# Delta rule in a twelve-stage decoder: block products of two units in one step, outputs copied out of PSUM at once, roots for two units together, decays by a scan

## The reference, cut to what matters

```python
q = silu(dwconv_causal(x @ Wq)); k = silu(dwconv_causal(x @ Wk)) * DK**-0.5; v = silu(dwconv_causal(x @ Wv))
alpha = sigmoid(x @ Wa + ba); beta = sigmoid(x @ Wb + bb)
def step(S, inp):                      # one token
    Sk = einsum('bhvk,bhk->bhv', S, kt)
    S = at * S - bt * (Sk - vt)[..., :, None] * kt[..., None, :]
    return S, einsum('bhvk,bhk->bhv', S, qt)
o = layernorm(outs) * sigmoid(x @ Wg)
return o @ Wo
```

## Time and profile before

| | before |
|---|---|
| median of 3 runs (lowest to highest) | 3912.71 us (3912.12 to 3914.6) |
| the profiled execution | 3915.85 us |
| its span | 3913.9 us |
| mean granted TensorE clock | 0.931 of full speed |
| PE busy | 3368.3 us, 86% |
| PEld busy | 2147.7 us, 55% |
| DVE busy | 2962.4 us, 76% |
| ACT busy | 1945.8 us, 50% |
| POOL busy | 1136.4 us, 29% |

### The profile page before, as it was taken

One profiled execution on the slowest core, in us unless ns is written; L12 is line 12 of the kernel. 1 busy time (PEld: TensorE's weight loads), 2 busy tenths in 40 slices (PEclk: granted clock), 3 DMA queues, 4 the chain that ended last, 5 costly groups with the idle time before them and its releaser, 6 DMA issues.

```text
span 3913.9 us, 63880 instructions
## 1 busy us (share of the span) xinstructions
PE 3368.3 (86%) x22787; PEld 2147.7 (55%) x22802; DVE 2962.4 (76%) x6366; ACT 1945.8 (50%) x4750; POOL 1136.4 (29%) x1183
## 2 busy tenths in 40 slices
PE   7799999999886296877989978788999999997765
PEld 3366666666554143664556655465666566664444
DVE  6798999989756867454367766768988888886668
ACT  4466666666552142431144434535666566663455
POOL 1633033215410200000011121113656565664110
PEclk9899999999997598988989998899999999998887
DMA  2222222222211010001000000112222222122000
GB/s 71 58 74 58 69 63 68 57 63 64 48 38 47 0 36 24 2 2 64 1 22 1 1 33 2 60 65 83 77 73 76 75 76 81 66 81 77 1 1 22
DMA packets 240232, 183.97 MB, mean 47 GB/s; under 512 B 117744, under 2 KB 216432, under 8 KB 239024
## 3 DMA queue, kind: packets, MB, share of 16 engines
q1 hardware_dynamic: 239920, 179.90, 15.2%
HBM read 164.61 MB, written 15.20 MB: 46 GB/s over the span
## 4 chain that ended last, share of the span: by engine, by line
PE 63%; DVE 26%; ACT 5%; issue 5%; SPq 0%; DMA 0%; POOL 0%; DVEq 0%; ACTq 0%; POOLq 0%
PE ps L310 22%; PE ps L3286 5%; PE ps L2912 3%; PE ps L3274 3%; PE ps L502 2%; PE ps L2958 2%; PE ps L580 1%; PE ps L2695 1%; DVE hMX L3031 1%; PE ps L3265 1%; PE ps L1972 1%; PE ps L2918 1%; PE ps L2171 1%; DVE daq L732 1%; PE ps L316 1%
## 5 line engine op out<-in xcount | busy, mean ns | idle before, releaser
L310 PE MATMUL ps<-xT,min 128*128 128x512 f32 (+1 forms) x1072 | 496.1, 608 | 11.8 <-DVE macc L3426 11.4
L3426 DVE SCALAR_TENSOR_TENSOR macc<-ps,mcw,macc 128x508 f32<-128x508 f32 (+2 forms) x408 | 302.6, 742 | 80.5 <-ACT macc L3353 70.8
L3527 POOL TENSOR_TENSOR mSQ<-mSQ,mtn 128x512 f32<-128x512 f32 x128 | 234.6, 1833 | 331.2 <-ACT mtn L3378 331.1
L310 PEld LDWEIGHTS ps<-xT,min 128*128 128x128 f32 (+1 forms) x1072 | 191.0, 189 | 228.2 <-issue 205.7
L3520 POOL TENSOR_TENSOR mE<-mE,mCB 128x1024 f32<-128x1024 f32 x128 | 302.2, 2361 | 44.4 <-DVE mE L3436 26.4
L3436 DVE TENSOR_TENSOR_SCAN mE<-mE,mid 128x1024 f32<-128x1024 f32 x128 | 300.1, 2344 | 0.0
L3031 DVE TENSOR_REDUCE hMX<-ps 128x2 f32<-128x512 f32 x256 | 165.4, 686 | 110.3 <-PE ps L2918 109.6
L3286 PE MATMUL ps<-mwo,macc 128*128 128x256 f32 x1024 | 243.0, 380 | 5.4 <-DVE macc L3443 5.3
L3374 ACT ACTIVATE mtn<-ps,mcol 128x64 f32<-128x64 f32 x1024 | 222.9, 334 | 2.8 <-PE ps L3265 2.8
L826 POOL TENSOR_TENSOR dTB<-did,dNB 128x1024 f32<-128x1024 f32 (+1 forms) x10 | 29.1, 2912 | 664.7 <-DMA dNB<-d_N 600.4
L2998 ACT ACTIVATE hE<-ps 128x512 f32<-128x512 f32 x256 | 139.0, 595 | 156.2 <-PE ps L2912 156.2
(11 more groups left out here) (597 smaller groups left out, 8261.2 us busy)
## 6 DMA issues: line engine op xcount, KB each, us to landing
mE<-m_decay SPq DMA_DIRECT2D x128, 512.0 KB, 3.5
dwk<-in_L_attn_Wk SPq DMA_DIRECT2D x64, 128.0 KB, 2.3
dwq<-in_L_attn_Wq SPq DMA_DIRECT2D x64, 128.0 KB, 2.3
dwv<-in_L_attn_Wv SPq DMA_DIRECT2D x64, 128.0 KB, 2.3
dwg<-in_L_attn_Wg SPq DMA_DIRECT2D x64, 128.0 KB, 2.4
dwo<-in_L_attn_Wo SPq DMA_DIRECT2D x64, 128.0 KB, 2.6
min<-in_m_in SPq DMA_DIRECT2D x2, 4096.0 KB, 18.2
d_N<-dNT SPq DMA_DIRECT2D x256, 16.0 KB, 1.5
```

Source lines behind the costliest of these rows:

```text
L310: t = pe.matmul(out, w[:, j, :], self.c.xT[:, j, blk(g, 512)], start=j == 0, stop=j == 1)
L3426: x = dve.scalar_tensor_tensor(out=acc[:, :, 3 - j:T], in0=p[:, :, 0:T - 3 + j], scalar=self.cw[:, i, j:j + 1], in1=acc[:, :, 3 - j:T], op ...
L3527: pool.tensor_tensor(self.SQ[g % 2][:, :], self.SQ[g % 2][:, :], self.tn[s][:, :], ALU.add).then_inc(*self.sqa.up)
```

## The change

- **Decays.** Alpha itself (an exponential) goes to DRAM once; each unit reads its row of 4 x 132 values into all partitions (`decay_in`), ACT scales an identity by beta's part of each column (`seed`), and DVE runs one scan over 528 elements, E(t) = alpha(t) E(t-1) + seed(t). The matmuls L509 and L510, the exponential L643 and the bf16 parts of the sums go.
- **Silu.** ACT takes Silu straight into KQ or av; the DVE step L739 goes. The gate stays a tanh.
- **Block products.** `p32` holds x32 of unit u and y32 of unit u-1, `p64` likewise x64 and y64, their matmuls interleaved. One group of y32 goes to bank 6.
- **Outputs.** `oc` copies bank 4 to SBUF right after `o`; the statistics read SBUF, and `on` works in place there, in a ring of three.
- **Roots.** `st` takes the statistics of each unit; `c1` and `c2` make the roots of two units (eight columns) in one chain, split over two iterations.
- **NB in two buffers.** The load of a batch waits for the batch before the last.
- **The rest.** LAG 13, a ring of 15, 85 iterations in place of 81, V and W in one buffer, the weights of v, gate and Wo in rings of four with a semaphore each, the write-out and read-back of the blocks moved ahead of the late weights in SP's list, the order of steps rewritten.

```diff
-        for t in range(self.U + self.LAG + 5):
-            a, b, v, w, x = t, t - 1, t - self.LAG, t - self.LAG - 1, t - self.LAG - 2
-            every = (("k", a), ("x32", v), ("vt", w), ("on", x), ("q", a), ("k2", a), ("y32", v), ("s0", b), ("w", w), ("s1", b), ("q2", a),
-                     ("v", v), ("x64", v), ("ot", x), ("gate", w), ("v2", v), ("y64", v), ("o", w), ("e", a), ("acc", x), ("close", x),
-                     ("stats", x - 1), ("scale", x - 2), ("turn", x - 3))
+        for t in range(self.U + self.LAG + 8):
+            a, b, v, w, x = t, t - 1, t - self.LAG, t - self.LAG - 2, t - self.LAG - 5
+            every = (("oc", w - 1), ("k", a), ("st", w - 1), ("c1", w - 1), ("c2", w - 2), ("p32", v), ("k1", a), ("on", x), ("q", a), ("vt", w),
+                     ("cols", a), ("s0", b), ("s1", b), ("k2", a), ("p64", v - 1), ("q1", a), ("seed", a), ("v", w + 1), ("ot", x), ("v0", w + 1),
+                     ("go", x), ("w", w), ("q2", a), ("gate", x + 1), ("v1", w + 1), ("e", a), ("acc", x), ("v2", w + 1), ("o", w),
+                     ("close", x), ("stats", x - 1), ("scale", x - 2), ("turn", x - 3))
...
# SP: one iteration of load()
+            if 0 <= b < self.U:
+                for m, u0 in enumerate(self.first):
+                    if b == u0:
+                        self.blocks_out(sp, m)
+                self.blocks_in(sp, b)
...
-                    if m:
-                        sp.wait_ge(*self.sub.at(m))
+            if m >= 2:
+                sp.wait_ge(*self.sub.at(m - 1))
...
+        if n + 4 < self.U:
+            self.decay_in(sp, n + 4)
...
+    def decay_in(self, sp, u):
+        row = self.decd[u // 16, u % 16, :].unsqueeze(0).broadcast_to([128, 528])
+        sp.dma_start(self.E[u % 4][:, :, :].rearrange("p j t -> p (j t)"), row).then_inc(self.e_sem[u % 4], 16)
...
# PE
-            elif step == "e":
...
-                pe.matmul(bank(6), self.sel[:, h:h + 1].broadcast_to([96, 128]), self.S3[:, blk(g, 512)], start=True, stop=False)
-                pe.matmul(g4(bank(6)), c.identb[:, :], bc(c.neg[:, :], 4), start=False, stop=True).then_inc(*self.eb.up)
...
+            elif step == "p64":
+                X, Y = u < self.U, u > 0
+                lo, hi = blk(0, 64), blk(1, 64)
+                if X:
+                    pe.wait_ge(*self.yc32.at(u + 1))
+                if Y:
+                    pe.wait_ge(*self.xc64.at(u))
+                    TT = g4(self.TT[(u - 1) % 4][:, :])
                 for b in range(4):
+                    to = slice(256 + 64 * b, 320 + 64 * b)
+                    if X:
+                        x = pe.matmul(bank(7)[hi, to], self.NT[r][lo, 128 * b + 64:128 * b + 128], self.T[u % 4][lo, b, :], start=True, stop=True)
+                    if Y:
+                        y = pe.matmul(bank(7)[lo, to], self.X2[1 - s][hi, b, :], TT[hi, b, hi], start=True, stop=True)
...
-                room[4] = self.on.at(u + 1)
+                room[4] = self.oc.at(u + 1)
...
# ACT
-                act.activation(self.tk[:, :], self.ak[:, :], ACT.Tanh, scale=0.5).then_inc(*self.hk.up)
+                act.activation(self.KQ[s][:, :, 0, :], g4(self.ak[:, :]), ACT.Silu).then_inc(*self.sk.up)
...
+            elif step == "seed":
                 for j in range(4):
-                    e = act.activation(self.E[s][:, j, 1:129], bank(6)[:, blk(j)], ACT.Exp, bias=self.col[:, 4 * g + j, h:h + 1])
+                    e = act.activation(self.seed[s][:, j, 1:129], c.ident[:, :], ACT.Copy, scale=self.col[:, 4 * g + j, h:h + 1])
...
+            elif step == "oc":
+                act.wait_ge(*self.o.at(u + 1))
+                if u >= 3:
+                    act.wait_ge(*self.ot.at(u - 2))
+                act.copy(self.O[u % 3][:, :], bank(4)).then_inc(*self.oc.up)
...
# DVE
+            elif step == "e":
...
+                dve.wait_ge(self.e_sem[u % 4], 16 * (u // 4 + 1))
+                dve.wait_ge(*self.sd.at(u + 1))
+                dve.tensor_tensor_scan(E, E, seed, 0.0, ALU.mult, ALU.add).then_inc(*self.de.up)
...
+            elif step == "c2":
+                st, (y, v, a) = self.s8[u // 2 % 2], [self.sw[u // 2 % 2][:, blk(i, 8)] for i in range(3)]
+                for _ in range(2):
+                    dve.wait_ge(own.sem, root)
+                    root = self.newton(dve, own, y, v, a)
...
+    def newton(self, dve, own, y, v, a):
+
+        dve.wait_ge(own.sem, own(dve.scalar_tensor_tensor(out=a, in0=y, scalar=-0.5, in1=y, op0=ALU.mult, op1=ALU.mult)))
+        dve.wait_ge(own.sem, own(dve.tensor_tensor(a, a, v, ALU.mult)))
+        return own(dve.scalar_tensor_tensor(out=y, in0=a, scalar=1.5, in1=y, op0=ALU.add, op1=ALU.mult))
...
# POOL
-            then(pool.tensor_tensor(TB, self.id32[0:P], NB.rearrange("p s t -> p t s"), ALU.subtract))
+            then(pool.tensor_scalar(TB, NB.rearrange("p s t -> p t s"), -1.0, 1.0, ALU.mult, ALU.mult))
+            then(pool.memset(TB.rearrange("p t c -> p (t c)")[:, 0:1024:33], 1.0))
```

More of the change, by code:

```diff
@@ new lines, in scores_out @@
+    def scores_out(self, sp, n):
+        m = self.batch[n]
+        sp.wait_ge(*self.nr.at(2 * n + 2))
+        if m >= 2 and n == self.first[m]:
+            sp.wait_ge(self.nb_sem[m % 2], 16 * (m // 2))
+        for k in range(4):
+            to = self.Nd[m % 2, n - self.first[m], :, k, :, :].rearrange("b s t -> s b t")
+            sp.dma_start(to, g4(self.NT[n % self.RING][blk(k, 32), :])[:, :, blk(k, 32)]).then_inc(self.n_sem[m % 2], 16)
+        if n == self.first[m] + self.BATCHES[m] - 1:
+            so_far = sum(self.BATCHES[i] for i in range(m % 2, m + 1, 2))
+            sp.wait_ge(self.n_sem[m % 2], 64 * so_far)
+            if m >= 2:
+                sp.wait_ge(*self.sub.at(m - 1))
+            P = 16 * self.BATCHES[m]
+            of = self.Nd[m % 2].rearrange("u b k s t -> (u b k) s t")[0:P]
+            sp.dma_start(self.NB[m % 2][0:P, :, :], of).then_inc(self.nb_sem[m % 2], 16)
+        if n + 4 < self.U:
+            self.decay_in(sp, n + 4)
@@ L495, in tensor @@
                 self.columns(pe, bank(b), w, g).then_inc(*done.up)
+            elif step == "cols":
+                pe.wait_ge(*room[4])
+                pe.wait_ge(*self.logs.at(1))
+                for j in range(4):
+                    t = pe.transpose(bank(4)[:, blk(j)], self.Bt[:, blk(j)], c.ident[:, :])
+                t.then_inc(*self.ab_tr.up)
+                room[4] = self.cols.at(1)
             elif step in ("s0", "s1"):
@@ new lines, in scalar @@
+                    e = act.activation(self.seed[s][:, j, 1:129], c.ident[:, :], ACT.Copy, scale=self.col[:, 4 * g + j, h:h + 1])
+                e.then_inc(*self.sd.up)
+            elif step == "p32":
+                p = bank(7).rearrange("p (i b n) -> p i b n", i=4, b=4)
+                if u:
+                    act.wait_ge(*self.y32.at(u))
+                if u < self.U:
+                    act.wait_ge(*self.x32.at(u + 1))
+                    act.copy(self.X[s][:, :, :], p[:, 0, :, :]).then_inc(*self.xc32.up)
+                if u:
+                    TT = g4(self.TT[(u - 1) % 4][:, :])
+                    for k in range(2):
+                        lo, hi = blk(2 * k, 32), blk(2 * k + 1, 32)
+                        act.activation(TT[lo, :, hi], p[lo, 0, :, :], ACT.Copy, scale=-1.0)
+                    act.activation(self.T[(u - 1) % 4][32:64, :, 0:32], bank(6)[32:64, 0:128].rearrange("p (b n) -> p b n", b=4), ACT.Copy, scale=-1.0).then_inc(*self.yc32.up)
+            elif step == "p64":
+                p = bank(7)[:, 256:512].rearrange("p (b n) -> p b n", b=4)
+                if u < self.U:
+                    act.wait_ge(*self.x64.at(u + 1))
+                    act.copy(self.X2[s][64:128, :, :], p[64:128]).then_inc(*self.xc64.up)
+                if u:
+                    act.wait_ge(*self.y64.at(u))
+                    act.activation(g4(self.TT[(u - 1) % 4][:, :])[0:64, :, 64:128], p[0:64], ACT.Copy, scale=-1.0).then_inc(*self.yc64.up)
@@ L708, in vector @@
+        then(dve.tensor_scalar(beta, bank(1), self.bia[:, 1:2], 0.0, ALU.add, ALU.min))
         dve.wait_ge(*self.soft.at(2))
-        dve.tensor_tensor(beta, beta, self.Bt[:, :], ALU.subtract)
-        then(dve.tensor_tensor(self.B1[:, :], self.B1[:, :], self.A[:, :], ALU.subtract))
-        for j in range(4):
-            x = dve.tensor_tensor_scan(self.cum[:, blk(j)], self.one[:, :], self.B1[:, blk(j)], 0.0, ALU.mult, ALU.add)
-        then(x)
-        dve.tensor_tensor(self.Bt[:, :], beta, self.cum[:, :], ALU.subtract).then_inc(*self.cummed.up)
```

364 lines of the change are left out of this document (164 added, 200 removed).

## The result

3799.6 us median (3798.3 to 3801.5, 4 runs) against 3912.4 in the same comparison: ratio 0.9711, 95% interval [0.9695, 0.9728]. Forecast 3804. The profiled execution took 3798.25 us, its span 3796.5. Behind the stage, where both kernels are the same, the two profiled executions differ by some 4.5 us (2735.5 from 1178.4 on, 2730.9 from 1065.6 on), so a few us of a single execution are not the change's.

What follows compares the result with a forecast made beforehand. PE bounds with POOL idle, DVE with POOL busy. The stage was to end at 134 + 52 + 6 + 708 + 166 = 1066 us against 1178; with a table load -111, forecast 3804 us, 8 in 10 range 3775 to 3868.

Steps and rivals of the forecast that it cites:

- from there to the first full iteration: After the first block product: five filling iterations, 52 us, plus 6 us of stall because batch 1 comes late from POOL.
- 46 full iterations: Iterations with all steps running: 46 at a mean of 15.4 us against 16.6 before, 708 us.
- tail: Late steps only: 15 iterations of PE's 9.6 plus 0.6 us, 153, then 13 for the last unit; 166 us.
- PE bounds the full iteration: Full iteration: PE's work falls from 16.16 to 15.0 us (14.56 to 15.72), 15.2 with handoffs and POOL idle.
- p64's overlap: Block products on PE: x64 and y64 run side by side, 0.61 us instead of 1.22 per iteration.
- Rival 1: Block products in p64 do not overlap: PE 15.7 us, 16.0 with handoffs, +37 us, 3841; chance 0.16.
- DVE: DVE's load per full iteration: 11.9 us with POOL idle, 13.5 with it busy, so it no longer bounds.
- My walk through the queues: Full iteration with POOL busy: q's copy and waiting for bank 3 make gate 0.9 us late; iteration 15.9 us.
- Front: Opening iterations where DVE sets the pace: still 7.2 us each, iteration 1 some 4 to 7 us earlier.
- Rival 2: ACT switches tables between Silu and tanh, two loads of 1.283 us per iteration: +79 us, 3883; chance 0.07.
- Rival 3: Slower than before: the serial loop through o, statistics, roots, k and v decides if handoffs cost more; 3933 at 18.2 us; chance 0.07.
- Rival 4: More than forecast: PE at 14.6 us and the scan hidden in POOL's phases, 46 x 0.8 less, 3767; chance 0.05.

Runs made afterwards that it cites:

- e2: Changed kernel plus two bf16 products of 512 columns per iteration on PE, ahead of v's transposes; 3818.0 us, ratio 0.9766.
- e1: Changed kernel with p64's four x64 products issued first and its four y64 products after, instead of alternating; 3815.3 us, ratio 0.9753.
- e5: Changed kernel plus three 128x512 DVE steps per iteration, after the taps of k, q and v, giving back the silu load; 3851.2 us, ratio 0.9851.
- e6: Changed kernel with e5's added steps and 13 more small dependent DVE steps per two units in the root chain; 3935.1 us, ratio 1.0061.
- e12: Kernel before the change with Silu alone on ACT for k, q and v, replacing tanh and a DVE step; 3889.2 us, ratio 0.9941.
- e3: Changed kernel with NB back in one buffer; 3807.3 us, ratio 0.9741.
- e10: Changed kernel with the residual norm in ten pieces, bank 6 copied first in p32, and c2 at the end of c1's iteration; 3769.3 us, ratio 0.9633.
- e9: Changed kernel with DVE's residual norm work cut into ten pieces spread over six iterations; 3785.8 us, ratio 0.9680.
- e8: Changed kernel with the copy out of bank 6 ahead of the two into TT, with its own signal; 3797.9 us, ratio 0.9711.
- e4: Changed kernel with the gate's tanh replaced by an exponential, whose function is in another table; 3819.5 us, ratio 0.9769.

## Why the prediction was right

The total was right to 0.1%, and the stage's end at 1066 to the microsecond. That exactness is luck: the terms were off by up to 27 us and cancelled. The direction, the bound and the size of most parts were not luck.

| term | predicted | measured |
|---|---|---|
| first block product | 133.6 | 127.0 |
| from there to the first full iteration | 52, and 6 of stall | 60.7, no stall |
| 46 full iterations | 708 | 685.8 |
| tail | 166 | 192.5 |

- **PE bounds the full iteration.** Right and shown (e2). Its size, 15.0 (15.4 with handoffs), was too high by 0.5: p64 came at 0.61 as taken; p32 at 0.49 (324.46 to 324.95 in e1's timeline) and not 0.64. Read from start to start in both kernels, x32 and y32 took 0.37 + 0.44 (y32 from 560.87 to 561.31) and not the chain's 0.75, so p32 saves 0.32 where I had 0.11. Terms that I left alone fell too: O by 0.10, the two transposes by 0.06 each, gate's product by 0.09. Together that is the 0.5. I had read a price on the chain of waits as the work itself. What made those pieces shorter was not tested.
- **p64's overlap.** Right in size and in most of the cause (e1): of the 0.61 some 0.45 are overlap by the estimate there, the rest comes from merging two short steps into one. The products of both halves go to bank 7, the case that the Trainium skill's "TensorEngine Tiling (Array Packing)" excludes under Restrictions and Gotchas; they write different partitions of it, and 16 in 0.61 us against 1.22 apart is the measurement that decides here. Rival 1 is out. (Its 15.7 for PE should read 15.6 by the prediction's own sum.)
- **DVE.** 12.1 and 12.7 us against 11.9 and 13.5: with POOL busy the root chain of eight columns came to 1.84 us where 2.2 was priced, and the scan of such an iteration to 1.26 where I had 1.2 x 3364/2282 = 1.77. I gave the iteration with POOL busy 15.9 us; it is 14.5. My walk through the queues charged 0.9 us for q's copy and the gate, of which the trace shows next to nothing (gate's product waits for q's taps 1.3 us in 45 iterations). That DVE's relief was necessary is shown from both sides (e5, e6, e12). PE's smaller work alone, in the kernel before, was not run; e6 is the nearest to it.
- **The mean.** 14.5 + 0.4: of the 20 us in 45 iterations 11 are two residual norms of 5.5 us, about 4 their neighbours (15.3 in place of 14.5), 2.4 a late batch of POOL at 233.6, where I had 2.5 us to spare, and about 2 three iterations of 15.0 to 15.4 from 769 to 843. The prediction had no term of its own for the norms, which cost 2.5 us each before (iterations of 18.6 beside 16.1); a slower iteration hid more of them.
- **Front.** 7.2 us an iteration as forecast. It starts at 28.7, 9.8 us earlier than the 38.5 of the earlier trace rows, where I had 4 to 7. Two buffers for NB are worth 6 to 8 us (e3).
- **The stall that did not come.** I had 6 us of stall for batch 1. Its first block product runs at 175.30 without a wait. The five filling iterations took 60.7 us in place of 52, at a mean granted clock of 0.92 and with 3.2 us of waiting for v's taps at 147.28. Two errors, 6 and 9 us, hide behind 58 against 60.7.
- **Tail: the step that failed.** I counted PE's 9.6 us and 0.6 for the copies of p32, 10.2 in all. Of 14 iterations, which average 11.6, every second waits for `on`, which waits for c2, and all wait 1.1 us in front of v's transposes; the last four units take 31.0 us, not 10.2 + 13. I had priced the tail by PE's work and one wait; what sets it are the waits for ACT's copies and for c2. Moving c2, with the norm split and the copies' order, took 17 us off the tail (e10); the norm alone gave 1.5 of them (e9), and the copies' order alone next to nothing (e8).
- **Rival 2.** It did not occur (the stage's last load is at 31.9 us), and it was wrongly priced: ACT's idle gaps take up most of the loads (e4).
- **Rival 3.** It did not occur. The loop through DVE can set the pace, but by its load and not by dearer handoffs: with DVE's load given back the kernel is slower than before although PE needs 14.5 us (e6). The change stays clear of it by the 1.7 us that DVE is idle in an iteration with POOL busy.
- **Rival 4.** Half of it came true: PE came below its 14.6 us, and the full iterations gave 22 of its 37 us. The tail took them back.

## What to carry to other kernels

Price each stage with the waits that it has itself: a step order that is hidden behind products in the full iterations is bare in the tail, and there a half chain in the wrong place costs every second iteration. A relief for an engine that is not the bound can still be what the gain rests on: give its load back and measure. A part of a change can be a loss by itself in the old order (`oc`, +13 us); what it is worth in the new one no run shows, since none takes it out of the changed kernel. Read prices of single steps from start to start in both kernels, and not once from the chain of waits and once from the timeline. When a total is right, compare its terms all the same: here 22 us too much in the full iterations covered 27 us too little in the tail.

## What the runs showed of the hardware

- The granted clock can fall behind idle time of PE, and that makes a stall cost more than its length. At 233.6 in the changed kernel PE had waited 2.39 us (for the blocks, by the code; the profile names no releaser) and went on at 1.00; at 233.97 in e10_roots_late it had waited 2.96 us, and the same products ran at 0.72, partly at the lower of the two levels (1.2 of 2.4 GHz):
```profile
233.60:237.00 3.40, 3.38 (x51) 2.28 (x52) 1.25 (x2) 2.69 (x9) 0.00 (x0) 1.00 0.61 140
```
```profile
234.40:237.00 2.60, 2.60 (x12) 0.95 (x6) 0.27 (x1) 2.33 (x8) 0.00 (x0) 0.72 0.57 121
```
That iteration took 19.2 us and the other 16.9: 0.6 us more of waiting, 2.3 us more in all. In e9_norm_split, after 2.98 us of waiting, the same products from 233.8 to 237.0 ran at 0.65.
- Small products on different row blocks overlap in part even when one block's are all issued first (e1).
- Two bf16 products of 512 columns among f32 ones took 0.43 us, nothing more for the change of type (e2).
